# A mixture-of-experts block: the first expert product in three 16 bit products instead of one in f32

## The reference

```python
x = layernorm(x + attention(x, W_Q, W_K, W_V))        # causal, one head
logits = (x @ gate_w + gate_b) / 0.9
# the best 2 of 8 experts a token, softmax over the two
h = gelu(einsum('bsd,edf->bsef', x, w1) + b1)         # w1: 8 x 128 x 512
expert_out = einsum('bsef,efd->bsed', h, w2) + b2     # w2: 8 x 512 x 128
out = einsum('bse,bsed->bsd', gate_probs, expert_out)
out = layernorm(out) * ln_g + ln_b
x = layernorm(x + out)
```

## Time and profile before

| | |
|---|---|
| three runs | 349.35, 349.51, 350.43 us (median 349.51) |
| profiled execution | 349.2 us, of which the span from the first to the last instruction is 347.3 |
| PE busy, share of the span | 266.2 us, 77% |
| POOL | 197.6 us, 57% |
| ACT | 195.7 us, 56% |
| DVE | 178.5 us, 51% |
| DMA | 41.94 MB, 121 GB/s in the mean |

### The profile page before, as it was taken

One profiled execution on the slowest core, in us unless ns is written; L12 is line 12 of the kernel. 1 busy time (PEld: TensorE's weight loads), 2 busy tenths in 40 slices (PEclk: granted clock), 3 DMA queues, 4 the chain that ended last, 5 costly groups with the idle time before them and its releaser, 6 DMA issues.

```text
span 347.3 us, 8074 instructions
## 1 busy us (share of the span) xinstructions
PE 266.2 (77%) x1993; PEld 234.9 (68%) x1994; DVE 178.5 (51%) x980; ACT 195.7 (56%) x579; POOL 197.6 (57%) x319
## 2 busy tenths in 40 slices
PE   2998897597876477874999999999999989960000
PEld 2576676386665376773999999999999879950000
DVE  0126784656786533421533333332457868952785
ACT  3247673565644383643678778653655678780241
POOL 8200068867875858688556555588878645560200
PEclk9999999789988879999699999999999999996555
DMA  5896112121222442221222335666598655016403
GB/s 145 268 332 131 32 55 78 46 63 39 78 85 85 121 116 58 68 63 49 69 61 77 92 92 156 198 182 186 165 365 283 163 140 187 23 47 201 139 0 91
DMA packets 45633, 41.94 MB, mean 121 GB/s; under 512 B 5520, under 2 KB 36416, under 8 KB 45600
## 3 DMA queue, kind: packets, MB, share of 16 engines
q1 hardware_dynamic: 41056, 32.20, 32.9%
q0 software_dynamic: 4544, 9.38, 7.9%
HBM read 26.00 MB, written 13.47 MB: 114 GB/s over the span
## 4 chain that ended last, share of the span: by engine, by line
PE 59%; DVE 10%; ACT 9%; issue 8%; another core or an unknown queue 7%; DMA 3%; DVEq 2%; SPq 1%; ACTq 1%; POOL 1%
PE bank L527 17%; PE bank L538 17%; PE bank L400 5%; PE bank L427 5%; ACT h L670 4%; PE bank L512 3%; PE bank L415 2%; PE bank L391 2%; PE bank L386 2%; PE bank L535 2%; DMA pair<-returned 1%; DVE sum_stats L928 1%; DVE negmax L734 1%; DMA wv<-in_L_attn_W_V_dram 1%
## 5 line engine op out<-in xcount | busy, mean ns | idle before, releaser
L670 ACT ACTIVATE h<-bank,b_cols 128x128 f32<-128x128 f32 x312 | 89.0, 373 | 57.6 <-PE bank L527 30.3
L1130 POOL DMA_INDIRECT returned<-x,slot_back x78 | 76.5, 981 | 53.0 <-DVE x L923 24.9
L527 PE MATMUL bank<-slot_xT,w_now 128*128 128x128 f32 x624 | 86.7, 283 | 6.4 <-ACT h L670 4.1
L538 PE MATMUL bank<-w_all,h 128*128 x624 | 88.7, 285 | 0.1
L527 PEld LDWEIGHTS bank<-slot_xT,w_now 128*128 128x128 f32 x624 | 79.4, 199 | 7.7 <-issue 7.0
L538 PEld LDWEIGHTS bank<-w_all,h 128*128 128x128 f32 x624 | 76.6, 193 | 1.3 <-issue 0.2
L1123 POOL DMA_INDIRECT slots<-rows,slot_of x64 | 62.5, 976 | 17.8 <-issue 14.2
L1116 POOL MEMSET pause_out<- 1x200 f32 x138 | 35.1, 254 | 44.9 <-DVE rows L837 44.4
L923 DVE TENSOR_SCALAR x<-bank,slot_gate 128x128 f32<-128x128 f32 x78 | 27.0, 348 | 47.7 <-PE bank L538 25.9
L680 ACT ACTIVATE pair<-pair,sum_shift,sum_rstd 128x128 f32<-128x128 f32 x60 | 25.3, 497 | 22.9 <-DVE sum_shift L946 22.9
L663 ACT ACTIVATE w_now<-w_all 128x512 f32 x40 | 25.9, 651 | 7.3 <-issue 7.3
(11 more groups left out here) (135 smaller groups left out, 327.5 us busy)
## 6 DMA issues: line engine op xcount, KB each, us to landing
w_now<-in_L_ffn_w_dram SPq DMA_DIRECT2D x38, 256.0 KB
slot_x<-slots SPq DMA_DIRECT2D x78, 65.0 KB
w_all<-in_L_ffn_w_dram SPq DMA_DIRECT2D x16, 256.0 KB, 5.7
pair<-returned SPq DMA_DIRECT2D x4, 640.0 KB
x<-n_L_attn_embeddings_dram SPq DMA_DIRECT2D x8, 256.0 KB, 4.0
rows<-rows SPq DMA_DIRECT2D x8, 256.0 KB, 3.8
pair<-returned SPq DMA_DIRECT2D x4, 384.0 KB, 5.3
out_dram<-pair SPq DMA_DIRECT2D x2, 640.0 KB, 8.7
```

What stands on the lines that cost most here:

```text
L527: m = nc.tensor.matmul(o, w1_now[:, s, cols], slot_xT[:, s % RING, :], start=True, stop=True)
L538: m = nc.tensor.matmul(o, h[:, s % RING, c * P:(c + 1) * P], w2_c, start=False, stop=(c == FC - 1))
L670: m = nc.scalar.activation(h[:, s % RING, cols], psH[s][:, cols], ACT.Gelu, bias=b1_cols[:, c:][:, bass.ds(first, 1)])
L1130: g_.indirect_dma_start(returned, bass.IndirectOffsetOnAxis(ap=slot_back[:, j:j + 1], axis=0), y[:, j % Y_RING, :], None).then_inc(y_retur ...
```

## The change

1. The expansion is three f16 products of halves. An f32 number is split into a high f16 part and what is left as a low f16 part, and w1 hi by x hi, w1 hi by x lo and w1 lo by x hi are summed in PSUM: 12 products of 16 bits a tile instead of 4 of f32. w1 (times 64) is split once at the start: ACT takes the high half of each expert (`take_w1_hi`), DVE the low half (`take_w1_lo`); its 8 loads stand ahead of those of x(1) and x(2). The rows are split once a batch, on ACT (`take_xn_hi`) and DVE (`take_xn_lo`), and are scattered as two halves in the same 512 bytes; `copy_rows` waits for the split. A tile's transpose is two f16 transposes.
2. Everything of an expert (w1 hi and lo, w2, one-hot, b1) lies in one block of the tensor `experts`, and one register a tile is its start. `w1_now`, `take_w1`, `load_w1` in the loop and their waits are gone. The products of `expand` now have addresses that depend on a register, too.
3. Bodies have 12 tiles, `slot_x` has 12 places, AHEAD is 3. `expand` waits for the gelu of tile j-3, `contract` for `weigh` of tile j-3 (a third bank), and PE's order in a tile is expand, transpose, contract.
4. `rsqrt_step` has 6 steps with a drain behind each, of 7 instructions. `add_ln_b` and `add_pair(1)` are DVE's instead of POOL's. The early units are 48 instead of 46 and start 4 tiles later, so that 10 of them stand behind the last tile; the second normalisation of set 0 on ACT moves there, too.

```diff
-UNROLL = 8
+UNROLL = 12
-AHEAD = 2
+AHEAD = 3
...
             def copy_rows(b):
                 tiles = slice(b * TB, (b + 1) * TB)
-                sp.wait_ge(xn_ready, b + 1)
+                sp.wait_ge(xn_split, b + 1)
...
-            def expand(i, s, late):
...
-                for c in range(FC):
-                    o, cols = psH[s][:, c * P:(c + 1) * P], slice(c * P, (c + 1) * P)
-                    m = nc.tensor.matmul(o, w1_now[:, s, cols], slot_xT[:, s % RING, :], start=True, stop=True)
+            def expand(j, s, at):
+                pe.wait_ge(slotT_ready, j + 1)
+                if not isinstance(j, int) or j > 2:
+                    pe.wait_ge(h_ready, j - 2)
+                x_hi, x_lo = slot_xT[:, s % XT_RING, 0:P], slot_xT[:, s % XT_RING, P:2 * P]
                 for c in range(FC):
+                    o = psH[s % 3][:, c * P:(c + 1) * P]
+                    w_hi, w_lo = (part_of(at, half + 2 * c * P, half + 2 * (c + 1) * P, F16) for half in (W1_HI, W1_LO))
+                    nc.tensor.matmul(o, w_hi, x_hi, start=True, stop=False)
+                    nc.tensor.matmul(o, w_hi, x_lo, start=False, stop=False)
+                    m = nc.tensor.matmul(o, w_lo, x_hi, start=False, stop=True)
...
+            def take_xn_hi(b):
+                act.wait_ge(xn_ready, b + 1)
+                nc.scalar.activation(xn_half(b, 0), x[:, b * TB:(b + 1) * TB, :], ACT.Copy).then_inc(xn_hi_ready, 1)
...
+            def take_xn_lo(b):
+                dve.wait_ge(xn_hi_ready, b + 1)
+                vec.tensor_tensor(xn_half(b, 1), x[:, b * TB:(b + 1) * TB, :], xn_half(b, 0), ALU.subtract).then_inc(xn_split, 1)
...
             def norm_and_choose(b, norm=True, choose=True):
                 c = b - 1
+                if choose:
+                    take_xn_lo(c)
...
             for j in range(RETURNS_AHEAD, J):
                 give_back(j)
-                if j == group_first[1] - 8:
-                    add_ln_b(0)
-                if j == group_first[1]:
-                    add_ln_b(1)
-                if j == ADD_AT:
-                    add_pair(1)
```

More of the change, by code:

```diff
@@ L222, in xn, with xn_half, part, part_of @@
         def xn(t):
-            return rows[:, 0, t, 0:D]
+            return x[:, t, :]
+        def xn_half(b, half):
+            return rows[:].bitcast(F16)[:, 0, b * TB:(b + 1) * TB, half * D:(half + 1) * D]
+        def part(start, end, dt):
+            return experts[:, :, start:end].bitcast(dt)
+        def part_of(at, start, end, dt):
+            return experts[:].rearrange("p e n -> p (e n)")[:, start:][:, bass.ds(at, end - start)].bitcast(dt)
         def returns_of(g):
@@ L548, in body @@
+                                                                skip_runtime_bounds_check_because="table_link() computes 0 .. E - 1 blocks")
+                return e
+            def body(i, first=False, last=False):
                 tiles = LAST if last else UNROLL
-                e = expert_numbers(i * UNROLL, tiles + LAG)
+                at = expert_blocks(i * UNROLL, tiles + LAG)
                 for s in range(tiles):
-                    if s + AHEAD < tiles:
-                        transpose_slots(i, s + AHEAD)
-                    elif not last:
-                        transpose_slots(i + 1, s + AHEAD - UNROLL)
-                    if not first or s >= LAG:
-                        contract(i * UNROLL + s - LAG, (s - LAG) % UNROLL, e[s])
-                    expand(i, s, late)
+                    expand(i * UNROLL + s, s, at[LAG + s])
@@ L563, in body @@
                         gate(B - 1)
-                    if first and s == 4:
+                    if first and s == 3:
                         prefix_sums(B - 1)
+                    if not last or s + AHEAD < LAST:
+                        transpose_slots(i, s + AHEAD)
+                    if not first or s >= LAG:
+                        contract(i * UNROLL + s - LAG, s - LAG + UNROLL, at[s])
+                if last:
+                    for s in range(tiles, tiles + LAG):
+                        contract(i * UNROLL + s - LAG, s - LAG + UNROLL, at[s])
             for s in range(AHEAD):
@@ L573, in _ @@
             with pe.Fori(BOUND, BODIES - 1) as i:
-                body(i, late=True)
-            body(BODIES - 1, late=True, last=True)
-            e = expert_numbers(J, LAG)
-            for s in range(LAG):
-                contract(J - LAG + s, (J - LAG + s) % UNROLL, e[s])
+                body(i)
+            body(BODIES - 1, last=True)
         @block.scalar
```

339 lines of the change are left out of this document (159 added, 180 removed).

## The result

The changed kernel takes 384.6 us (median of 4 runs, 383.9 to 387.5), the kernel before 349.5 on the same chip: the ratio is 1.105, with a 95% interval from 1.099 to 1.112. The forecast was 339 us, faster. The profiled execution of the changed kernel took 385.0 us, 383.2 of them in the span; before it was 349.2 and 347.3.

What follows compares the result with a forecast made beforehand. It took PE to bound the quiet stretch (2.05 us a tile), and PE's instruction stream after the change. Terms -3 - 5 - 5 + 3 + 1 - 1.6 = -10.6 on 349.2 gave 339 us, range 328 to 351.

Steps and rivals of the forecast that it cites:

- the price of a register instruction: PE's stream in a tile: 0.10 us each, 15 take 1.5 to 1.8, with a semaphore 1.87 us, above the array's 1.78.
- The rival: PE's tile, slower case (chance 0.12): 0.13 us a register instruction would also give the deciding pace of 2.17 us.
- -3 stood for both: PE's pace including body starts: 2.00 us a tile against 2.05, over some 60 tiles -3 us.
- The 0.1 for a semaphore: PE's stream in a tile: about 0.1 us for a semaphore, added to the 15 register instructions.
- The start of a body: PE at each body's start, nothing queued: 1.3 to 1.6 us for 12 tiles, 0.12 a tile.
- 16 bit products: PE's expansion: 0.056 us a product with the weight load hidden, 12 take 0.67 us instead of 0.89 for f32.
- The rival of 0.081: PE's expansion: weights don't load under 16 bit products, 0.081 us each, tile 2.23, 353 us, slower; chance 0.12.
- POOL's work, -5 us: Late tiles: additions move from POOL to DVE, so the 5.4 us lost there go; -5 us (0 to -6).
- Banks, ring and order, -5 us: Stretch with remote waits: three open tiles cover single late releases of ACT; half of 10, -5 us (0 to -10).
- the case named against it: Same stretch: if releases come late one after another, their rate counts and the third open tile doesn't help.
- Front, +3 and +1: Before the tiles: splitting rows delays `prefix_sums` by 0.64 us in five batches, +3 (0 to +5); splitting w1 +1 (0 to +3).
- End, -1.6: Behind the last tile, on DVE: four 1/sqrt with fewer drained steps, -1.6 us; ten early units fit under an 8.38 us wait.

Runs made afterwards that it cites:

- e2: Changed kernel with PE always taking expert 0's block, so its products have fixed addresses and no register loads: 321.7 us, ratio 0.952 to the kernel before.
- e1: Changed kernel with the expert's number in the table instead of the byte offset, multiplied once a tile on PE and ACT: 336.2 us against 339.1 before, ratio 0.994.
- e7: e1 without the second product of each chunk (high weights by low tokens), same register instructions: 342.6 us, one run, against 346.3 before.
- e10: e1 with ACT copying the expert's two w1 halves to a fixed place two tiles ahead: 331.6 us against 340.1 before, ratio 0.975.
- e11: e1 with the additions of ln_b back on POOL, in two portions among the returns: ratio 0.997 to the kernel before.
- e9: The changed kernel as it is, run again on the chip of e8, e10 and e11: 374.9 us against 340.1 before, ratio 1.102.
- e8: The program of e1 run again, on the chip of e9, e10 and e11: 336.9 us against 340.1 before, ratio 0.990.
- e4: Changed kernel with the table in units of 2 bytes, so nine of 13 register instructions a tile have three steps, no divide: 356.0 us, ratio 1.053 to before.
- e3: Kernel before with a zero register added to the offset of the contraction's five products, giving longer addresses: 343.1 us, ratio 1.015, two runs.
- e5: e1 with PE's 15 registers of a body loaded in three pieces (7, 4 and 4): 346.9 us against 346.3 before, ratio 1.001.
- e6: e1 with bodies of 18 tiles, 21 registers a load and a ring of six transposed tiles: 345.6 us, ratio 0.998 to before.

## Why the prediction was wrong

**The step that failed** is the price of a register instruction: "What one costs can be seen only where PE has run dry ... 0.10 us each", and from it "15 take 1.5 to 1.8 us ... I take 1.87". The form of the argument was right. The stream, not the array, sets the pace; the array takes 1.78 (e2); a 16 bit product 0.056. With addresses of one step the two numbers come out near the 1.78 and 1.87 foretold: 1.78 (e1, e2) and 1.80 to 2.00 (e7). But the 0.10 to 0.12 had been read on instructions of one and two steps, and the changed kernel's have four, one of them a divide: 0.163. I had counted rows that say only ISA and not looked at what they hold. 13 x (0.163 - 0.112) = 0.66, which turns the 1.81 of such a stream into 2.47. The rival named the road ("0.13 us a register instruction ... 2.17") with too small a figure. Over 60 tiles it is 60 x (2.47 - 2.00) = +28 us, and +39 with the starts of bodies, where -3 stood for both.

The trace's record of such an instruction is 78 to 80 ns shorter than the distance to the next (32 and 112, 37 and 115, 85 and 163), the same for each length; what fills these 78 to 80 ns no run shows. The 0.1 for a semaphore is near what the traces have: the record of such a wait on PE lasts 51 ns, and the next instruction starts 0.105 us or more behind its start, before and in the changed kernel.

**The start of a body.** Foretold were 1.3 to 1.6 us for 12 tiles, read on ACT's idle time of 1.29. ACT's own load in that row's place lasts 1.80 us, and PE's load of 11 registers in the kernel before 1.32; the trace had both. It is 2.4 to 2.7 at four starts and 1.3 at the last, 11.6 us in tiles 17 to 77 for 2.9 before. The load is 1.66 us, wait and branch come to it, and of the clock's fall behind the gap the prediction said nothing. In the changed kernel the fall is nearly free: the start of tile 48, behind which the clock stayed at 1.00, cost 4.72 + 2.82 - 2 x 2.47 = 2.6 us, those of tiles 24, 36 and 60, behind which it fell, 2.4 to 2.7; in e1 it is the difference between starts of 3.7 and 4.2 us and one of 2.5 behind a gap as long.

**16 bit products.** 0.056 us in a stream of loads and products, both with register instructions of one step between them that PE is through with in time (e1) and without (e10). The rival of 0.081 falls.

**POOL's work, -5 us.** The late tiles no longer lose the 5.4 us: POOL follows DVE. But a tile of 2.47 us would also give it room, and with tiles near 1.8 us the additions on POOL (e11) come with a loss of some 2.4 us, which the trace doesn't tie to them. And 2.3 of the 5.4 us were not POOL's to begin with. They lie in tiles 68 and 69 of the kernel before, where DVE waited for ACT's normalised rows (L680) and PE's next transpose for DVE's copy, while POOL itself stood waiting for DVE:

```profile
283.02 0.82 DVE L953 TENSOR_TENSOR pair<-pair,lng 128x640 f32<-128x640 f32 x1 [2.52 <-ACT pair L680]
284.22 0.33 PE L512 MATMUL bank<-ident,slot_x 128*128 128x128 f32 x1 [1.27 <-DVE slot_xT L915]
285.18 1.00 POOL L1130 DMA_INDIRECT returned<-x,slot_back  x1 [3.59 <-DVE x L923]
```

So the loss was gone as forecast, but its cause was only in part the one named, and no run shows what POOL's share was. In e1 tiles 62 to 71 take 1.8 to 2.2 us: most at the pace of the stream, 67 to 70 with waits for DVE, which then works at the early units.

**Banks, ring and order, -5 us.** None of it can be seen: tiles 0 to 17 take 55.2 us for 53.5, and 50.4 in e9. The same tiles take 46.9 us even where PE has no register instructions (e2), though 17 at its pace would take 30.3, so releases that come late one after another still rule there. That was the case named against it. What the third bank is worth wasn't tried.

**Front, +3 and +1.** `prefix_sums` comes 0.59 us later, as foretold (0.64); tile 0 starts only 1.4 us later, within the scatter of several us from trace to trace, so neither the +3 nor the +1 can be told from nothing. **End, -1.6:** -1.1. The ten early units did fit under the wait, of which 1.66 of 8.38 us are left.

Sum by these sizes: +1.4 + 1.7 + 28.2 (pace) + 11.1 (starts and tiles of 2.5 to 2.6, less the 2.9 before) - 5.4 (late tiles) - 1.1 = 35.9 us.

## What to carry over

Where short products draw their addresses from registers, add up the engine's instruction stream beside its array, and price a register instruction by the steps it holds, not by its kind: here one of one or two steps came every 0.112 to 0.115 us, one of four with a divide every 0.163. Look for a divide in the addresses: with the expert's number times a constant in the register (e1) there was none, and this one small edit was worth 38 us (e8 against e9). In e1 the stream (1.80 us a tile and more) was no faster than the array (1.78), and behind loads of 15 registers the products' starts stood 1.53 to 2.07 us apart; in e10, where ACT's copy took the expansion's addresses off PE, the array had products queued, and at the start of tile 24 it stood idle for 0.90. And read where a loss lies, tile by tile and wait by wait, before a change is credited with taking it away.

## What the runs showed of the hardware

- On PE the record of a register instruction grew with its steps: 32 ns for one and 37 for two (before, e1), 46 for three (e4), 85 for four with a divide (changed kernel; 85 to 96 in e3 and e4), mostly 160 for five with a divide (e3); to the next one 78 to 80 ns more.
- Loads of registers on PE, from 150 us on: 0.5 us for 2 and 1.0 to 1.1 for 4 (e5), 1.3 to 1.5 for 11 (kernel before), 1.6 to 1.8 for 15 (changed kernel, e1, e7), but 0.85 to 1.00 for 9 in the last body (changed kernel, e1, e11); and 5.2 and 5.1 for 21 at two places of e6. Neither is explained.
- The clock fell to 0.50 for 3.4 us behind gaps of 2.02 and 2.07 us (e1, tiles 24 and 48) and three of 2.16 to 2.26 in the changed kernel, but not behind 1.99 (e1, tile 60) or 2.28 (changed kernel, tile 48). Over all traces it fell at 17 of the 25 starts of bodies (tiles 24 to 60) with a gap of 1.95 to 2.33 us and at none of those with 1.9 or less; away from a start it fell once behind a gap of 1.54 (e3, at 280 us). So the gap's length alone doesn't tell.
- PE is shown as busy for 12.00 of 12.00 us (250 to 262 us of the changed kernel) though its 16 bit products start 0.06 to 0.16 us apart, where in e1 they start 0.056 apart; PEld is busy for 9.21 of these 12.00 us, in e1 for 15.89 of 16.00 (193 to 209).
- The same program (the kernel before) has medians of 339 to 350 us on four chips. The two traces of the changed kernel are 12.3 us apart (383.2 and 370.9), all of it ahead of tile 17.
